# Attention by pairs of heads, with the value matmuls of four heads in four column groups

## The chip, the cores and the metric

The kernel runs on one core of one Trainium2 chip, in one launch. The metric is the device time of that launch in microseconds (us); less is better.

## The reference

One input, 4 images of 16 x 16 tokens with 192 channels (1024 tokens in all), goes through three stages, each added to its input, all in 32-bit floats:

1. a group norm, then a mixture of 8 experts (two a token, inner size 512) with a shared expert;
2. a layer norm, then attention with 12 heads of 16 channels over the 256 tokens of an image;
3. a layer norm, then a mixture of 16 experts (two a token, inner size 384) with a shared expert.

The attention, in which the change lies, takes two softmaxes, the second over the masked result of the first:

```
qkv = einsum('bnc,fc->bnf', x, w_qkv)                       # -> q, k, v
att = softmax(einsum('bhxd,bhyd->bhxy', q, k) * 16**-0.5)
att = softmax(att * mask)                                   # mask: 0.5 where x = y modulo 64, else 1
out = einsum('bhxy,bhyd->bhxd', att, v)
return einsum('bnc,oc->bno', out, w_out) + b_out
```

## The kernel before

The program is written engine by engine: each engine has one fixed order of instructions, and semaphores (`wait_ge`, `then_inc`) tie the orders together. An engine that waits holds up everything behind the wait in its own order. The order around the change is written out by hand, as a loop over steps n on each engine.

There are 48 heads (12 for each of 4 images), counted through as n. For each of them:

- `scores` (TensorE): q and k, split beforehand into high and low parts, are multiplied for two heads at once. A head's 32 rows lie in one of four row groups, and the matmuls of the two heads alternate. The result, 2 x 128 queries by 256 keys, takes one of PSUM's banks 0 to 3.
- `neg_maximum` (VectorE) takes the negated maxima of each query, `exp_scores` (ScalarE) the exponentials and their sums into one of three buffers `e1`.
- `attention` (VectorE): a reciprocal of the sums and two multiplies, which give the normalised and masked weights in one of two buffers `att`. After each a semaphore is counted up for TensorE.
- `att_transpose` (TensorE): four blocks of 128 x 128 are transposed into bank 4 or 5 by turns; the two on the diagonal as plain matmuls with the identity (L1320), the two others in the engine's own transpose mode (L1322). In the trace a plain matmul of 32-bit floats is two records, a transpose is one.
- `exp_att` (ScalarE): the exponential of the second softmax, into one of three buffers `p2_t`.
- `weigh_values` (TensorE, L1333): two matmuls, one for each half of the keys, with the head's 32 columns of values as the stationary side and 256 queries as the moving one. Head n writes partitions 32 (n mod 4) to 32 (n mod 4) + 31 of bank 6, that is, it uses one of four column groups of the array. One more column of ones gives the sum for the second softmax.

Four heads make a chunk. `out_copy` (ScalarE) takes bank 6 out; `sums_by_token` (TensorE, L1350), `invert_sums` (VectorE), a copy on GpSimd (L522), `spread_inverses` (TensorE, L1358) and `out_norm` (VectorE) divide by the sums; each third chunk `project` (TensorE, L1368) and `residual` (VectorE) finish an image. `chunk_at` says in which step a chunk's turn comes.

What each engine does in step n:

```
TensorE: scores(n+1) and (n+2) in one (n odd); att_transpose(n-2); weigh_values(n-3); chunk's parts
VectorE: neg_maximum(n); attention(n-1); chunk's parts
ScalarE: exp_scores(n); exp_att(n-2); out_copy
```

Ahead of the attention lie its layer norm, the projections to q and k (L1275) and to v (L1304); behind it the next layer norm, whose transposes (L1257) and matmuls (L1097) begin the third stage. Weights of that stage are loaded by SyncE's queue: a middle part of them is started when `sc_ps` shows that the last scores are in PSUM.

Of the kernel before, what the change touches and what calls it, by code (L numbers as in the profile page):

```python
# [29 lines left out]
P = 128  # L30
# [4 lines left out]
CH = 96  # L35
# [94 lines left out]
def build(nc, d, out):  # L130
    with ExitStack() as ctx:
# [109 lines left out]
        xn_t = sb("xn_t", [CH + 1, NCH, T])  # L241
# [53 lines left out]
        g_sh = [sb(f"g_sh{i}", [P, 512]) for i in range(2)]  # L295
# [3 lines left out]
        neg_max = sb("neg_max", [P, 4, 2])  # L299
        exp_sum = sb("exp_sum", [P, 4, 2])  # L300
        exp_inv = sb("exp_inv", [P, 2, 2])
# [3 lines left out]
        e1 = [scratch_at(512 * i, 2, TOKENS_IMG) for i in range(3)]  # L305
        att = [scratch_at(512 * (3 + i), 2, TOKENS_IMG) for i in range(2)]
        p2_t = [scratch_at(512 * (5 + i), 2, TOKENS_IMG) for i in range(3)]
# [55 lines left out]
        SUMS = 7  # L363
        TAIL = 3
        ATT_STEPS = N_HEADS + SUMS + 3 - TAIL

        def chunk_at(n, lag):


            last = N_HEADS // HPC - 1  # L370
            if lag >= SUMS and n == N_HEADS - 1 + lag - TAIL:
                return last
            c = (n - lag + 1) // HPC - 1
            return c if (n - lag + 1) % HPC == 0 and 0 <= c < last + (lag < SUMS) else None

        def sums_bank(c):

            return 0 if c == N_HEADS // HPC - 1 else 7


# [29 lines left out]
        def _(sp):  # L410
# [39 lines left out]
            sp.wait_ge(sc_ps, N_HEADS)  # L450
# [55 lines left out]
        def _(pool):  # L506
# [11 lines left out]
            for c in range(N_HEADS // HPC):  # L518
# [74 lines left out]
        def _(act):  # L593
# [32 lines left out]
            def exp_scores(n):  # L626
                act.wait_ge(nmax_ready, n + 1)
                if n >= 3:
                    act.wait_ge(att_ready, n - 2)
                for qt in range(2):  # L630
                    nc.scalar.activation(e1[n % 3][:, qt, :], bank[:, n % 4, qt * 256:(qt + 1) * 256], ACT.Exp,  # L631
                                         bias=neg_max[:, n % 4, qt:qt + 1],
                                         accum_out=exp_sum[:, n % 4, qt:qt + 1]).then_inc(e1_ready, 1)

            def exp_att(n):
                act.wait_ge(att_t_ps, n + 1)
                if n >= 3:
                    act.wait_ge(av_ps, n - 2)
                nc.scalar.activation(p2_t[n % 3][:].rearrange("p a b -> p (a b)"), bank[:, 4 + n % 2, :],
                                     ACT.Exp).then_inc(p2_ready, 1)  # L640

            def out_copy(c):

                act.wait_ge(av_ps, HPC * (c + 1))
# [28 lines left out]
        def _(dve):  # L673
# [272 lines left out]
            def neg_maximum(n):  # L946
                dve.wait_ge(sc_ps, n + 1)
                v.tensor_reduce(neg_max[:, n % 4, :], bank[:, n % 4, :].rearrange("p (a b) -> p a b", a=2),  # L948
# [12 lines left out]
            def attention(n):  # L961

                dve.wait_ge(e1_ready, 2 * n + 2)
                if n >= 2:

                    dve.wait_ge(att_t_ps, n - 1)
                go(v.reciprocal(exp_inv[:, n % 2, :], exp_sum[:, n % 4, :]))
                for qt in range(2):
                    ins = v.scalar_tensor_tensor(att[n % 2][:, qt, :], e1[n % 3][:, qt, :], exp_inv[:, n % 2, qt:qt + 1],  # L969
                                                 mask, ALU.mult, ALU.mult)  # L970
                    if qt == 0:
                        step(ins)
                ins.then_inc(att_ready, 1)

            def invert_sums(c):
                dve.wait_ge(sums_ps, c + 1)
                if c:
                    dve.wait_ge(wide_ready, c)
                v.reciprocal(o_inv[:].rearrange("p a h -> p (a h)"),   # L979
                             bank[:, sums_bank(c), 0:2 * HPC]).then_inc(inv_ready, 1)  # L980

            def out_norm(c):
# [5 lines left out]
                v.tensor_tensor(o_t[:, c % HC, :], o_raw[:, c % 2, :], bank[:, sums_bank(c), 0:TOKENS_IMG], ALU.mult  # L988
# [8 lines left out]
            for n in range(ATT_STEPS):  # L997
                if 2 <= n < N_HEADS:
                    neg_maximum(n)
                if 0 <= n - 1 < N_HEADS:  # L1000
                    attention(n - 1)
                if n == N_HEADS:

                    ln_stats(0)
                if chunk_at(n, SUMS) is not None:
                    invert_sums(chunk_at(n, SUMS))
                if n == ATT_STEPS - 1:
                    ln_rows(2, 0)
                if chunk_at(n, SUMS + 2) is not None:
                    out_norm(chunk_at(n, SUMS + 2))  # L1010
                if (chunk_at(n, SUMS + 3) or 0) % HC == HC - 1:
                    residual(chunk_at(n, SUMS + 3) // HC)
# [445 lines left out]
```

## Time and profile before

| | us |
|---|---|
| three runs | 549.63, 543.4, 545.7 |
| their median | 545.7 |
| span of the profiled execution | 538.7 |
| TensorE busy in it | 477.6 (89%) |
| VectorE busy in it | 235.1 (44%) |
| ScalarE busy in it | 162.4 (30%) |

The span goes from the first to the last instruction of one execution, taken by the hardware profiler. Its own time isn't recorded apart from it; the runs' times hold what lies around the span as well. PE is TensorE's matmuls, PEld its weight loads, DVE VectorE, ACT ScalarE, POOL GpSimd. A line such as L1333 is a line of the kernel before.

### The profile page before, as it was taken

Reading aid. Unit: us, or ns where it says so; the run is one execution under the profiler, and the core shown is the slowest. Engines: PE = TensorE matmul, PEld = TensorE weight load, DVE = VectorE, ACT = ScalarE, POOL = GpSimd, SP = SyncE. Lnnn points to the kernel's source line nnn. Section 1 sums busy time; section 2 is a strip of 40 time slices with the busy share of each in tenths; the row PEclk is TensorE's granted clock in tenths of the full one; section 3 lists DMA queues with packets and bytes.
Section 4 is the critical chain, followed back from the end, with each engine's and each line's share of the span. In section 5 each row is a group of like instructions: output and inputs, shape, how many; then the busy total and the mean of one; then the engine's idle time right before and its main releaser. Section 6 shows DMA issues by size and latency. Waiting matters only on the chain.

```text
span 538.7 us, 7851 instructions
## 1 busy us (share of the span) xinstructions
PE 477.6 (89%) x2343; PEld 322.5 (60%) x2344; DVE 235.1 (44%) x676; ACT 162.4 (30%) x418; POOL 152.3 (28%) x135
## 2 busy tenths in 40 slices
PE   0999999999998169899999999889999999999990
PEld 0554766565656147766676666655767666666660
DVE  5157232222222344676666665638623333333330
ACT  2142002111112023466656565442012111121210
POOL 2000115556655100000000000000125565566652
PEclk9999699999999669899999999999899999999996
DMA  9992111222220593000000003764211221221100
GB/s 265 209 350 67 35 52 23 39 38 35 39 27 9 141 331 135 1 1 0 2 1 1 1 2 83 181 174 112 77 38 31 33 25 26 34 35 23 12 0 0
DMA packets 20956, 36.20 MB, mean 67 GB/s; under 512 B 6544, under 2 KB 17481, under 8 KB 20484
## 3 DMA queue, kind: packets, MB, share of 16 engines
q1 hardware_dynamic: 10468, 29.56, 19.3%
q0 software_dynamic: 10464, 6.33, 8.4%
q8 instruction: 13, 0.21, 0.2%
q14 instruction: 11, 0.09, 0.1%
HBM read 31.92 MB, written 8.45 MB: 75 GB/s over the span
## 4 chain that ended last, share of the span: by engine, by line
PE 69%; DMA 15%; DVE 6%; issue 5%; ACT 1%; POOL 1%; POOLq 1%; SPq 0%; DVEq 0%
PE bank L1158 15%; DMA sum<-y,slot_tok 12%; PE bank L1333 9%; PE bank L1097 8%; PE bank L1173 6%; PE bank L1320 6%; PE bank L1127 4%; PE bank L1275 4%; PE bank L1289 3%; PE bank L1165 2%; PE bank L1322 2%; PE bank L1368 2%; PE bank L1134 1%; PE bank L1079 1%; PE bank L1304 1%
## 5 line engine op out<-in xcount | busy, mean ns | idle before, releaser
L473 POOL DMA_INDIRECT rows<-xn_rows,slot_tok x56 | 58.4, 1042 | 131.5 <-DVEq L800 90.6
L1158 PE MATMUL bank<-w_first,rows_t 96*128 x248 | 85.4, 487 | 0.2 <-issue 0.2
L1173 PE MATMUL bank<-w_second,hid_t 128*128 x370 | 71.4, 333 | 8.3 <-issue 6.3
L859 DVE TENSOR_SCALAR y<-bank,slot_w 128x192 f32<-128x192 f32 x54 | 22.6, 418 | 102.5 <-PE bank L1173 83.6
L1173 PEld LDWEIGHTS bank<-w_second,hid_t 128*128 128x128 f32 x370 | 58.7, 190 | 13.5 <-issue 13.1
L484 POOL DMA_INDIRECT out<-y,slot_tok x31 | 48.9, 1577 | 47.4 <-DMA out<-y,slot_tok 28.2
L1158 PEld LDWEIGHTS bank<-w_first,rows_t 96*128 96x128 f32 x248 | 44.6, 190 | 25.5 <-issue 0.7
L631 ACT ACTIVATE scratch<-bank,neg_max 128x256 f32<-128x256 f32 x96 | 44.6, 470 | 39.2 <-DVE neg_max L948 34.4
L1333 PE MATMUL bank<-scratch,w_first 128*32 128x256 f32 x192 | 50.9, 390 | 0.0
L522 POOL COPY act_h<-o_inv 128x256 f32<-128x256 f32 x12 | 4.8, 400 | 162.7 <-DVE o_inv L979 162.0
L484 POOL DMA_INDIRECT sum<-y,slot_tok x23 | 36.3, 1577 | 36.3 <-DMA sum<-y,slot_tok 23.7
L1152 PE MATMUL bank<-w_first,rows_t 96*128 (+1 forms) x92 | 43.4, 593 | 0.1
L1320 PE MATMUL bank<-const,scratch 128*128 128x128 f32 x192 | 42.1, 302 | 1.1 <-DVE scratch L969 1.1
L969 DVE SCALAR_TENSOR_TENSOR scratch<-scratch,exp_inv,const 128x256 f32<-128x256 f32 x96 | 42.3, 482 | 1.7
L852 DVE TENSOR_TENSOR act_h<-bank,act_g 128x384 f32<-128x384 f32 x31 | 17.3, 558 | 57.9 <-PE bank L1158 57.9
L569 ACT COPY rows_t<-bank 96x256 f32<-96x256 f32 x56 | 20.5, 365 | 64.1 <-PE bank L1134 63.8
L580 ACT ACTIVATE act_g<-bank 128x384 f32<-128x384 f32 x31 | 15.2, 490 | 75.1 <-PE bank L1158 75.1
L1320 PEld LDWEIGHTS bank<-const,scratch 128*128 128x128 f32 x192 | 29.4, 192 | 13.0 <-DVE scratch L969 5.3
L575 ACT ACTIVATE act_h<-bank 128x512 f32<-128x512 f32 x23 | 13.7, 597 | 76.7 <-PE bank L1152 76.7
L1097 PE MATMUL bank<-xn_t,w_first 96*128 96x512 f32 x64 | 31.6, 640 | 3.5 <-DVE xn_t L700 3.5
L847 DVE COPY hid_t<-bank 128x384 f32<-128x384 f32 (+1 forms) x54 | 32.9, 610 | 3.7 <-PE bank L1165 3.4
L948 DVE TENSOR_REDUCE neg_max<-bank 128x2 f32<-128x512 f32 x48 | 32.4, 676 | 2.8 <-PE bank L1289 2.3
(172 smaller groups left out, 649.3 us busy)
## 6 DMA issues: line engine op xcount, KB each, us to landing
w_first<-in_gate_up SPq DMA_DIRECT2D x16, 576.0 KB
w_second<-in_down SPq DMA_DIRECT2D x1, 4608.0 KB, 24.5
w_first<-in_fc SPq DMA_DIRECT2D x1, 3072.0 KB
w_second<-in_fc SPq DMA_DIRECT2D x1, 3072.0 KB, 28.5
xn_rows<-xn_tok SPq DMA_DIRECT2D x2, 768.0 KB, 5.9
rows<-xn_rows,slot_tok POOLq DMA_INDIRECT x56, 2.7
w_first<-in_x_t SPq DMA_DIRECT2D x2, 384.0 KB, 4.4
w_first<-in_w SPq DMA_DIRECT2D x1, 768.0 KB, 7.0
```

The source lines that it names most:

```text
L473: pool.indirect_dma_start(rows[b % 2][:], None, xn_rows[L.l], bass.IndirectOffsetOnAxis(slot_tok[:, b:b + 1].bitcast(U32), 0), bounds_chec ...
L484: pool.indirect_dma_start(target, bass.IndirectOffsetOnAxis(slot_tok[:, b:b + 1].bitcast(U32), 0), y[b % 2][:], None, bounds_check=T - 1, ...
L631: nc.scalar.activation(e1[n % 3][:, qt, :], bank[:, n % 4, qt * 256:(qt + 1) * 256], ACT.Exp, bias=neg_max[:, n % 4, qt:qt + 1], accum_out ...
L847: v.tensor_copy(hid_t[:, 0:L.I], bank[:, 7, 0:L.I]).then_inc(L.hid_t_ready, 1)
L948: v.tensor_reduce(neg_max[:, n % 4, :], bank[:, n % 4, :].rearrange("p (a b) -> p a b", a=2), AXX, ALU.max, negate=True).then_inc(nmax_rea ...
L969: ins = v.scalar_tensor_tensor(att[n % 2][:, qt, :], e1[n % 3][:, qt, :], exp_inv[:, n % 2, qt:qt + 1], mask, ALU.mult, ALU.mult)
L1097: ins = pe.matmul(bank[:, bk + s % 2, :], w[:, k, g, ic * P:(ic + 1) * P], xn_t[0:CH, k, half * HALF:(half + 1) * HALF], start=(k == 0), s ...
L1152: ins = pe.matmul(bank[:, 5, :], rows_t[0:kr, k, :], w(kr, k * I0, I0), start=(k == 0), stop=(k == NCH - 1))
L1158: ins = pe.matmul(bank[:, 5 + g, 0:I1], rows_t[0:CH, k, :], w(CH, (k * 2 + g) * I1, I1), start=(k == 0), stop=(k == NCH - 1))
L1173: ins = pe.matmul(bank[:, 1, 0:C], hid_t[:, tile(ic)], w(P, ic * C, C), start=(ic == 0), stop=(ic == L.IC - 1))
L1320: ins = pe.matmul(dst, src, ident, start=True, stop=True)
L1333: ins = pe.matmul(bank[g * HG:(g + 1) * HG, 6, 0:TOKENS_IMG], v_tok[:, 2 * img + kt, h, :], p2_t[n % 3][:, kt, :], start=(kt == 0), stop=( ...
```

## The change

Every step of the attention now treats a pair of heads, p = 0 to 23:

- `scores(p)` writes two banks, 0 and 1 or 2 and 3, and counts its semaphore once.
- `neg_maximum(p)` is one instruction over both heads' banks (1024 columns), `exp_scores(p)` four activations with one count, `attention(p)` one reciprocal and four multiplies. They write in place, into `e1`, of which there are three of twice the size; `att` is gone.
- `att_transpose(p)` transposes eight blocks into banks 4 and 5 together, with no second pair of banks; the diagonal blocks stay plain matmuls with the identity. `exp_att(p)` is one activation over both banks.
- `weigh_values(c)` does a chunk's four heads in one go: for each half of the keys the four heads one after another, each in its own column group.
- The sums of a chunk go to columns of bank 6 behind the values, and the spread inverses always to bank 7. The last chunks' parts are written out behind the loops.
- The three buffers `p2_t` of a pair lie in the scratch area, in `xn_t` (now 128 partitions high) and in the two `g_sh` as one.

What each engine does in step p is now:

```
TensorE: scores(p+2); att_transpose(p); weigh_values (p even); chunk's parts
VectorE: neg_maximum(p+2); attention(p); chunk's parts
ScalarE: exp_scores(p+2); exp_att(p); out_copy
```

The core of the diff:

```diff
-            def exp_scores(n):
-                act.wait_ge(nmax_ready, n + 1)
-                if n >= 3:
-                    act.wait_ge(att_ready, n - 2)
-                for qt in range(2):
...
+            def exp_scores(p):
+                act.wait_ge(nmax_ready, p + 1)
+                if p >= 3:
+                    act.wait_ge(att_t_ps, p - 2)
+                for q in range(4):
...
+                ins.then_inc(e1_ready, 1)
+
+            def exp_att(p):
+                act.wait_ge(att_t_ps, p + 1)
+                if p >= 3:
+                    act.wait_ge(av_ps, (p - 3) // PAIRS_CHUNK + 1)
+                nc.scalar.activation(p2_t[p % 3].rearrange("p a b -> p (a b)"),
+                                     bank[:, 4:6, :].rearrange("p a b -> p (a b)"), ACT.Exp).then_inc(p2_ready, 1)
...
             act.wait_ge(v_ps, NT // 2)
-            for n in range(N_HEADS + 3):
-                if n < N_HEADS:
-                    exp_scores(n)
-                if 0 <= n - 2 < N_HEADS:
-                    exp_att(n - 2)
-                if chunk_at(n, 3) is not None:
-                    out_copy(chunk_at(n, 3))
+            exp_scores(0)
+            exp_scores(1)
+            for p in range(N_PAIRS):
+                if p + 2 < N_PAIRS:
+                    exp_scores(p + 2)
+                exp_att(p)
+                if chunk_at(p, 1) is not None:
+                    out_copy(chunk_at(p, 1))
+            out_copy(N_CHUNKS - 1)
...
-            def attention(n):
-
-                dve.wait_ge(e1_ready, 2 * n + 2)
-                if n >= 2:
-
-                    dve.wait_ge(att_t_ps, n - 1)
-                go(v.reciprocal(exp_inv[:, n % 2, :], exp_sum[:, n % 4, :]))
-                for qt in range(2):
-                    ins = v.scalar_tensor_tensor(att[n % 2][:, qt, :], e1[n % 3][:, qt, :], exp_inv[:, n % 2, qt:qt + 1],
+            def attention(p):
+
+                dve.wait_ge(e1_ready, p + 1)
+                go(v.reciprocal(exp_inv[:, p % 2, :], exp_sum[:, p % 4, :]))
+                for q in range(4):
+                    ins = v.scalar_tensor_tensor(e1[p % 3][:, q, :], e1[p % 3][:, q, :], exp_inv[:, p % 2, q:q + 1],
                                                  mask, ALU.mult, ALU.mult)
...
+            for p in range(N_PAIRS):
+                if p + 2 < N_PAIRS:
+                    neg_maximum(p + 2)
+                attention(p)
+                if chunk_at(p, 2) is not None:
+                    invert_sums(chunk_at(p, 2))
+                if chunk_at(p, 3) is not None:
+                    out_norm(chunk_at(p, 3))
+                if (chunk_at(p, 4) or 0) % HC == HC - 1:
+                    residual(chunk_at(p, 4) // HC)
...
+            def scores(p):
+
+                pair, img = (2 * p, 2 * p + 1), 2 * p // HEADS
+                if p >= 2:
+                    pe.wait_ge(e1_ready, p - 1)
...
+            def att_transpose(p):
+                pe.wait_ge(att_ready, p + 1)
+                if p:
+                    pe.wait_ge(p2_ready, p)
+                for m in range(2):
+                    for kt in range(2):
+                        for qt in range(2):
+                            dst = bank[:, 4 + m, (kt * 2 + qt) * P:(kt * 2 + qt + 1) * P]
+                            src = e1[p % 3][:, 2 * m + qt, tile(kt)]
+                            if kt == qt:
+
+                                ins = pe.matmul(dst, src, ident, start=True, stop=True)
+                            else:
+                                ins = pe.transpose(dst, src, ident)
+                ins.then_inc(att_t_ps, 1)
+
+            def weigh_values(c):
+                pe.wait_ge(p2_ready, PAIRS_CHUNK * (c + 1))
+                if c:
+
+                    pe.wait_ge(o_raw_ready, c)
+                    pe.wait_ge(inv_ready, c)
+                img = c // HC
                 for kt in range(2):
...
+                    for g in range(HPC):
+                        p = c * PAIRS_CHUNK + g // 2
+                        ins = pe.matmul(bank[g * HG:(g + 1) * HG, 6, 0:TOKENS_IMG],
+                                        v_tok[:, 2 * img + kt, (c % HC) * HPC + g, :], p2_t[p % 3][:, 2 * (g % 2) + kt, :],
+                                        start=(kt == 0), stop=(kt == 1))
                 ins.then_inc(av_ps, 1)
...
+            for p in range(N_PAIRS):
+
+                if p + 2 < N_PAIRS:
+                    scores(p + 2)
+                att_transpose(p)
+                if chunk_at(p, 1) is not None:
+                    weigh_values(chunk_at(p, 1))
+                if chunk_at(p, 2) is not None:
+                    sums_by_token(chunk_at(p, 2))
+                if chunk_at(p, 3) is not None:
+                    spread_inverses(chunk_at(p, 3))
+                if (chunk_at(p, 4) or 0) % HC == HC - 1:
+                    project(chunk_at(p, 4) // HC)
+            weigh_values(N_CHUNKS - 1)
+            spread_inverses(N_CHUNKS - 2)
+            sums_by_token(N_CHUNKS - 1)
+            spread_inverses(N_CHUNKS - 1)
+            project(IMAGES - 1)
```

## Rows read from the trace of the kernel before

**Rows 1.** The page: an engine's busy time; a costly group of VectorE.

```profile
PE 477.6 (89%) x2343; PEld 322.5 (60%) x2344; DVE 235.1 (44%) x676; ACT 162.4 (30%) x418; POOL 152.3 (28%) x135
...
L969 DVE SCALAR_TENSOR_TENSOR scratch<-scratch,exp_inv,const 128x256 f32<-128x256 f32 x96 | 42.3, 482 | 1.7
```

**Rows 2.** Busy time by stretch: stretch, its length, busy (instructions) by engine, clock, DMA.

```profile
223.00:350.00 127.00, 124.30 (x787) 82.48 (x788) 86.22 (x233) 77.97 (x254) 4.80 (x12) 0.99 0.11 29
...
222.80:226.20 3.40, 2.13 (x22) 1.81 (x22) 2.83 (x8) 2.56 (x11) 0.00 (x0) 1.00 0.00 0
...
226.20:229.70 3.50, 3.50 (x14) 1.89 (x10) 3.43 (x10) 3.21 (x12) 0.00 (x0) 0.51 0.00 0
...
55.60:59.00 3.40, 3.40 (x11) 2.53 (x10) 0.36 (x1) 0.00 (x0) 1.04 (x1) 0.50 0.21 53
```

**Rows 3.** The chain of waits: start us, length us, what.

```profile
202.34 12.56 PE bank L1275 x54
...
261.12 0.98 PE bank L1333 x4
...
270.73 0.98 PE bank L1333 x4
271.71 2.15 PE bank L1368 x12
...
342.68 1.74 PE bank L1333 x8
```

**Rows 4.** The timeline of TensorE, one chunk: start us, length us, what.

```profile
259.15 0.44 PE L1358 MATMUL bank<-const,act_h 128*128 128x128 f32 x2
259.52 0.39 PE L1289 MATMUL bank<-k_high,q_parts 32*128 32x256 f32 x2
...
259.97 0.29 PE L1289 MATMUL bank<-k_low,q_parts 32*128 32x256 f32 x2
260.19 0.49 PE L1320 MATMUL bank<-const,scratch 128*128 128x128 f32 x2
260.51 0.38 PE L1322 MATMUL bank<-const,scratch 128*128 128x128 f32 x2
260.73 0.39 PE L1320 MATMUL bank<-const,scratch 128*128 128x128 f32 x2
261.05 1.05 PE L1333 MATMUL bank<-scratch,w_first 128*32 128x256 f32 x4
262.03 0.49 PE L1320 MATMUL bank<-const,scratch 128*128 128x128 f32 x2
...
263.87 0.61 PE L1350 MATMUL bank<-const,w_first 128*128 128x4 f32 x4
264.41 0.39 PE L1289 MATMUL bank<-k_high,q_parts 32*128 32x256 f32 x2
```

**Rows 5.** The timeline at the attention's start.

```profile
223.87 0.88 DVE L969 SCALAR_TENSOR_TENSOR scratch<-scratch,exp_inv,const 128x256 f32<-128x256 f32 x2
...
224.80 0.49 PE L1320 MATMUL bank<-const,scratch 128*128 128x128 f32 x2 [0.84 <-DVE scratch L969]
```

**Rows 6.** The timeline of VectorE in one step.

```profile
264.64 0.64 DVE L948 TENSOR_REDUCE neg_max<-bank 128x2 f32<-128x512 f32 x1
265.20 0.15 DVE L967 RECIPROCAL exp_inv<-exp_sum 128x2 f32<-128x2 f32 x1
265.39 0.88 DVE L969 SCALAR_TENSOR_TENSOR scratch<-scratch,exp_inv,const 128x256 f32<-128x256 f32 x2
```

**Rows 7.** The timeline of ScalarE in one step.

```profile
265.32 0.47 ACT L631 ACTIVATE scratch<-bank,neg_max 128x256 f32<-128x256 f32 x1 [0.97 <-DVE neg_max L948]
...
266.23 0.59 ACT L639 ACTIVATE scratch<-bank 128x512 f32<-128x512 f32 x1
```

**Rows 8.** The timeline of TensorE at the low clock.

```profile
226.39 0.79 PE L1320 MATMUL bank<-const,scratch 128*128 128x128 f32 x2
...
227.97 1.87 PE L1333 MATMUL bank<-scratch,w_first 128*32 128x256 f32 x4
```

More of the change, by code:

```diff
@@ L362, in build, with chunk_at @@
         N_HEADS = IMAGES * HEADS
[L363 to L378, printed above, removed]
+        N_PAIRS = N_HEADS // 2
+        N_CHUNKS = N_HEADS // HPC
+        PAIRS_CHUNK = HPC // 2
+        def chunk_at(p, lag):
+            c = (p - lag + 1) // PAIRS_CHUNK - 1
+            if c == N_CHUNKS - 1 or (p - lag + 1) % PAIRS_CHUNK or c < 0 or c >= N_CHUNKS:
+                return None
+            return c
+        SUMS_AT = TOKENS_IMG
         HALF = T // 2
@@ L448, in _ @@
             sp.dma_start(w_second[:], d["down"]).then_inc(s_w1b, 16)
-            sp.wait_ge(sc_ps, N_HEADS)
+            sp.wait_ge(sc_ps, N_PAIRS)
             for e in range(EARLY, MIDDLE):
@@ L516, in _ @@
             pool_blocks(pool, L0, sum0)
-            for c in range(N_HEADS // HPC):
+            for c in range(N_CHUNKS):
                 pool.wait_ge(inv_ready, c + 1)
@@ L995, in residual @@
                 dve.sem_inc(x_new, 1)
[L997 to L1012, printed above, removed]
+            for p in range(N_PAIRS):
[8 more added lines that the diff above has]
+                    residual(chunk_at(p, 4) // HC)
+            ln_stats(0)
+            out_norm(N_CHUNKS - 2)
+            invert_sums(N_CHUNKS - 1)
+            ln_rows(2, 0)
+            out_norm(N_CHUNKS - 1)
+            residual(IMAGES - 1)
             ln_stats(1)
@@ L1325, in weigh_values @@
-            def weigh_values(n):
-                img, h = n // HEADS, n % HEADS
-                g, c = n % HPC, n // HPC
-                pe.wait_ge(p2_ready, n + 1)
-                if g == 0 and c:
-                    pe.wait_ge(o_raw_ready, c)
-                for kt in range(2):
-                    ins = pe.matmul(bank[g * HG:(g + 1) * HG, 6, 0:TOKENS_IMG],
-                                    v_tok[:, 2 * img + kt, h, :], p2_t[n % 3][:, kt, :],
-                                    start=(kt == 0), stop=(kt == 1))
+            def att_transpose(p):
[12 more added lines that the diff above has]
+                ins.then_inc(att_t_ps, 1)
@@ L1340, in sums_by_token, with spread_inverses @@
                 pe.wait_ge(o_raw_ready, c + 1)
-                if sums_bank(c) == 0:
-                    pe.wait_ge(e1_ready, 2 * N_HEADS)
-                elif c and c % HC == 0:
+                for qt in range(2):
+                    o = SUMS_AT + qt * HPC
+                    ins = pe.matmul(bank[:, 6, o:o + HPC], o_raw[:, c % 2, tile(qt)], sum_row,
+                                    start=True, stop=True)
+                ins.then_inc(sums_ps, 1)
+            def spread_inverses(c):
+                pe.wait_ge(wide_ready, c + 1)
+                if c and c % HC == 0:
                     pe.wait_ge(x_new, c // HC)
@@ L1348, in sums_by_token @@
                 for qt in range(2):
-                    o = qt * HPC
-                    ins = pe.matmul(bank[:, sums_bank(c), o:o + HPC], o_raw[:, c % 2, tile(qt)], sum_row,
-                                    start=True, stop=True)
-                ins.then_inc(sums_ps, 1)
-            def spread_inverses(c):
-                pe.wait_ge(wide_ready, c + 1)
-                for qt in range(2):
-                    ins = pe.transpose(bank[:, sums_bank(c), tile(qt)], o_inv_wide[:, qt].rearrange("p g d -> p (g d)"), ident)
+                    ins = pe.transpose(bank[:, 7, tile(qt)], o_inv_wide[:, qt].rearrange("p g d -> p (g d)"), ident)
                 ins.then_inc(spread_ps, 1)
```

80 lines of the change are left out of this document (24 added, 56 removed).

## The prediction

> **What bounds the kernel now.** I began with the page's shares [rows 1]: TensorE is busy for 89% of the span. The page says nothing of which stage the change sits in, so the next view is the busy time by stretch. Between 223 and 350 us, the attention, TensorE is busy 124.30 of 127.00 us, VectorE 86.22 and ScalarE 77.97, at a granted clock of 0.99 [rows 2]. TensorE alone is the bound there, and what it does all the time must be priced step by step. The chain of waits gives the rhythm: the same value matmuls come back at 261.12 and 270.73, so a chunk of four heads takes 9.61 us [rows 3]. The timeline of TensorE then splits one such chunk [rows 4]: a pair's scores take 0.67 us to the next step (259.52 to 260.19), the six transpose records of one head 0.86 (to 261.05), the value matmuls of one head 0.98 (to 262.03), the sums 0.54 (263.87 to 264.41) and the spreading of the inverses 0.37 (259.15 to 259.52). 2 x (0.67 + 2 x 0.86 + 2 x 0.98) + 0.54 + 0.37 = 9.61: the pieces fill the period, and there is no hole in it. A projection adds 2.15 us once for each image [rows 3].
>
> Why there is no hole matters more than the sizes. In the loop before, TensorE transposes head n-2 in the step in which VectorE normalises head n-1, and the scores are two to three heads ahead of the maxima. Each engine works on something that the other finished a step ago.
>
> **What the change takes away on TensorE.** Transposes: twelve records in a row instead of twice six, so one change of kind of work less. A pair of records costs 0.22 us (260.51 to 260.73 [rows 4]), so twelve take 0.86 + 6 x 0.11 = 1.52 against 1.72: 0.2 us a pair is gained.
>
> Values: the same sixteen records a chunk, two for each matmul (four for the two matmuls of a head in the row at 261.05). One costs 1.74 / 8 = 0.218 us [rows 3], and the switch 0.98 - 4 x 0.218 = 0.11. No row shows two column groups at work at once, so the cost is bounded. One after the other: 16 x 0.218 + 0.11 = 3.60 us a chunk, against 3.92 now. All four at once: 4 x 0.218 + 0.11 = 0.98. The nearest rows are those of the scores, whose pairs lie in two row groups: four couples of 256-column matmuls start within 0.45 us (259.52 to 259.97, three steps of 0.15 a couple [rows 4]), while 96-row matmuls of 512 columns in the same number format take 12.56 / 54 = 0.233 us each, 0.116 for 256 columns and 0.233 for two [rows 3]. So two groups do run at once. But the order matters: each value matmul is two records in the same column group, one behind the other, and matmuls start in order. The second record of group 0 has to wait for the first, group 1 can then join it, and so on: at most two at once, 9 slots for 16 records, 9 x 0.218 + 0.11 = 2.07 us. I take that, as it follows from the rows of the scores, and keep both ends for the range.
>
> The page "TensorEngine Tiling (Array Packing)" of the Trainium skill (Theoretical Speedup) gives up to four times for 32 columns. By it the values would cost 0.98 us a chunk, 1.09 less than in my sum.
>
> On TensorE alone a chunk would be 2 x (0.67 + 1.52) + 2.07 + 0.91 = 7.36 us, a gain of 2.25 us in each of twelve. That is the gain the page of the profile invites one to book, and I don't think that it comes.
>
> **What the change adds: a loop through two engines with no step of slack.** Follow the new order. In step p TensorE issues the scores of pair p+2, then the transposes of pair p. VectorE in step p takes the maxima of pair p+2, then normalises pair p. The maxima wait for those scores. The transposes of p wait for the normalisation of p, which stands behind the maxima of p+2 in VectorE's order. The scores of p+3 stand behind the transposes of p in TensorE's order. So: transposes of p, scores of p+3, maxima of p+3, normalisation of p+1, transposes of p+1. Nothing of this overlaps. TensorE waits during all of VectorE's part and VectorE waits during all of TensorE's; the value matmuls, sums, spreads and projections stand between transposes and scores and lie wholly on the path, too. One pair's round, with the clock at 2.4 GHz:
> - scores, first start to last end: 259.52 to 259.97 + 0.29 = 0.74 us [rows 4];
> - handing over to VectorE and back 0.05 each (normalisation 223.87 + 0.88 = 224.75, transposes at 224.80 [rows 5]);
> - maxima of 1024 columns: 0.56 for 512 (264.64 to 265.20 [rows 6]), and the further 512 columns at no more than that; 1.10;
> - reciprocal to first multiply 0.19 (265.20 to 265.39 [rows 6]), then four multiplies: two take 0.88 in all [rows 6], one alone 0.48 [rows 1], so each further one adds 0.40: 0.88 + 2 x 0.40 = 1.68;
> - transposes 1.52.
> Sum 0.74 + 0.10 + 1.10 + 0.19 + 1.68 + 1.52 = 5.33 us a pair, 10.7 a chunk before values, sums and spreads, where all of it takes 9.61 now.
>
> Start: the first transposes are at 224.80 [rows 5]. They now come after two more exponentials (0.91, half of a pair's four, 265.32 to 266.23 [rows 7]), a pair's scores (0.79 with the handover), the maxima (1.10) and two more multiplies (0.80): 228.4. From there 23 rounds to the last transposes: 21 x 5.33 = 111.9; two without scores and maxima, 2 x 3.44 = 6.9; eleven times values, 22.8; eleven sums, 5.9; ten spreads, 3.7; three projections, 6.5. Together 157.7, so they start at 386.1. Before they start at 342.68 - 0.86 = 341.8 [rows 3]. The tail behind them grows by 0.66 (six more records), 0.35 (one exponential over both heads; four exponentials of 256 columns and one of 1024 are some 2.8 us a pair and hidden in the loop) and 0.3 (2.07 instead of 1.74): 1.3. At full clock the span grows by 44.3 + 1.3 = 45.6 us.
>
> **The clock.** The start of the attention is a small picture of the new loop: from 222.8 to 226.2 us TensorE does scores, waits 0.84 us for a normalisation, transposes; it is busy 2.13 of 3.40 us, and in the next stretch its granted clock is 0.51, that is 1.2 GHz [rows 2, 5]. In the new loop it waits 3.1 us of every 5 to 8. I expect the clock to fall over and over. How quickly it returns is open: one fully busy stretch sufficed after 226.2, while from 55.6 to 59 us it stayed at 0.50 with TensorE busy 3.40 of 3.40 [rows 2]. At the low level six transpose records take 1.58 instead of 0.86 (226.39 to 227.97) and four value records 1.87 instead of 1.05 [rows 8]. Then the scores cost 1.14, the twelve transposes 2.9, the round 7.11, the short round 4.82, the values 4.1, sums, spreads and projections twice theirs: 149.3 + 9.6 + 45.1 + 19.2 + 12.9 = 236.1 instead of 157.7, with 6.7 more in the tail: 85 us on top if nothing ran at 2.4 GHz. A chunk has one long busy stretch (transposes, values, spread, scores: some 9 us at the low level), in which the clock should return, and two pauses, in which it falls. I take six tenths of TensorE's work at the low level: 45.6 + 0.6 x 85 = 97 us. This share is a choice between the ends, not a reading.
>
> **Parts that cost nothing.** Normalising in place, dropping the separate buffers, the wider rooms for two tensors and single increments change no term. The load of the middle experts' weights waits for the last scores as before, and is covered by the same 40 us of routing and shared expert behind the attention; without that cover it would be as late as now. The bank that holds a pair's transposes is no longer doubled: its exponential, near 0.95 us, is done during scores and VectorE's part (3.9 us). ScalarE has 2.8 us of work in a round of 5.3.
>
> **The sum.** The profiled execution's span is 538.7 us, 7.0 below the median of 545.7 of the three runs; what lies around the span doesn't change, so the difference is added to the median: 545.7 + 97 = 643 us.
>
> **Rivals.**
> 1. The clock holds, because the pauses are short: 545.7 + 45.6 = 591. For it: the attention's granted clock was 0.99 over 127 us, and no row shows what the clock does when short pauses and bursts alternate for long. Against it: the start of this very stage [rows 2]. 0.25.
> 2. It falls once and stays low: 545.7 + 131 = 677. For it the stretch at 55.6. 0.13.
> 3. The column groups don't overlap at all: 1.5 us more a chunk at full clock, 3 at low, about 27 more than my forecast: 670. 0.08. Four at once: 1.1 to 2.2 less a chunk, 623. 0.08.
> 4. The other side: TensorE passes a waiting matmul, and starts the scores of pair p+3 while the transposes of pair p still wait. Then the loop is cut, TensorE's 7.36 us a chunk (above VectorE's 2 x (1.10 + 0.19 + 1.60) + 0.6 = 6.4, the 0.6 being the two short steps that a chunk has beside its pairs) set the time, and the gain is 2.25 x 11 = 25 us: 521. It decides as soon as the scores can go before the wait. No row shows a matmul that started ahead of an earlier one; weight loads do stand ahead of matmuls. 0.04. The page "TensorE: Matmul & The Clock Gate" of the Trainium skill (Part 3, What overlaps and what doesn't) says that matmuls start and end strictly in order, which speaks against this one.
> My forecast has the remaining 0.42.
>
> **Range and chances.** 585 to 688 takes in rival 1 with its nearest variants, rivals 2 and 3, and leaves out the fourth and the corner of four groups at once with a full clock (578). A difference under 1% can't be told from none here (the three runs spread over 6 us). Faster by over 1%: 0.03; within 1%: 0.02, for a mixture of small pauses that I can't construct; slower: 0.95.
>
> **What will show it.** TensorE's busy share in the attention falls from 98% to some 55 to 65%, and nearly all of its idle time ends with the normalisation's multiply; VectorE's idle time ends with the scores. The chain of waits shows VectorE with a third or more of the attention, where it hardly appears now. The attention lasts 170 to 255 us. If value records of different groups start in pairs 0.22 us apart, two at once is right; if a chunk's sixteen start within 1 us, four. The granted clock should show many changes between the levels. I am wrong if scores are seen to start before the waiting transposes, or if the clock stays at one level throughout.

## The result and the profile after

The changed kernel takes 627.0 us (median of four runs), against 547.7 for the kernel before beside it: a ratio of 1.149 (95% interval 1.142 to 1.157), slower by 15%. Here and below the medians take in all executions; some executions of one and the same kernel have a lower granted clock throughout and take 1 to 3% longer, and the ratios leave these out. The profiled execution took 625.9 us, with a span of 623.8.

The page of the changed kernel, its engines' totals, the granted clock and the shares of the chain that ended last:

```profile
PE 485.3 (78%) x2343; PEld 346.7 (56%) x2344; DVE 231.4 (37%) x628; ACT 161.0 (26%) x394; POOL 152.5 (24%) x135
...
PEclk9998799999985955787966676666999999999997
...
PE 60%; DVE 16%; DMA 15%; issue 6%; ACT 2%; POOLq 1%; POOL 0%; SPq 0%; DVEq 0%
```

TensorE has the same 2343 matmul records as before [rows 1] and is busy 8 us longer, yet the span is 85 us longer. So most of the time went into waiting. VectorE holds 16% of the last chain, 6% before, and the clock row has a ragged middle. The busy time of the whole attention and of its first 34 us (stretch, length, busy time and instructions by engine, clock, DMA):

```profile
223.00:430.00 207.00, 129.37 (x789) 104.91 (x788) 82.29 (x184) 76.85 (x230) 4.83 (x12) 0.68 0.08 18
...
223.00:257.00 34.00, 20.35 (x109) 17.11 (x108) 12.72 (x25) 13.89 (x48) 0.00 (x0) 0.54 0.00 0
```

TensorE is busy 129.37 of 207 us where it was 124.30 of 127 [rows 2], and the granted clock is 0.68 instead of 0.99. Everything behind the attention is as before: the next stage's first matmul stands at 351.51 before and at 436.85 now, 187 us from the end of the span in both. The chain of waits of the changed kernel shows the loop that the prediction spelt out, here from the value matmuls of one chunk through the next transposes, and the value matmuls a chunk later:

```profile
298.91 1.00 PE bank L1340 x16
299.91 0.37 PE bank L1362 x2
300.28 0.69 PE bank L1293 x8
...
300.99 1.22 DVE neg_max L955
302.21 0.10 DVE exp_inv L971
...
302.74 1.28 DVE scratch L973 x3
...
304.06 0.49 PE bank L1325 x2
...
314.23 1.86 PE bank L1340 x16
```

Values, spread inverses, scores, maxima, reciprocal, multiplies, transposes follow each other (the first multiply is in a row left out). Nothing overlaps: in the timeline TensorE is idle for 3.11 us before the transposes at 304.06, and VectorE for 4.39 us before 300.32, when the inverses are spread. Compare the chunk at 261.12 [rows 3], where the value matmuls ended the waits and VectorE didn't appear. The list of waits says the same from both sides:

```profile
PE bank L1325 <- DVE scratch L973: 73.6, 24, 3.2
DVE w_first L992 <- PE bank L1362: 49.7, 10, 5.5
...
DVE o_inv L983 <- PE bank L1350: 37.0, 12, 3.7
...
DVE neg_max L955 <- PE bank L1293: 22.4, 21, 5.9
```

TensorE waits for the normalisation in each of the 24 rounds, 3.1 us on average. VectorE's waits are for the spread inverses, the sums and the scores, all made by TensorE in the same step.

The values are where the profile disagrees with the prediction. TensorE's timeline of one chunk:

```profile
298.84 0.41 PE L1340 MATMUL bank<-scratch,w_first 128*32 128x256 f32 x2
298.85 0.41 PE L1340 MATMUL bank<-xn_t,w_first 128*32 128x256 f32 x2
299.08 0.38 PE L1340 MATMUL bank<-scratch,w_first 128*32 128x256 f32 x2
299.09 0.39 PE L1340 MATMUL bank<-xn_t,w_first 128*32 128x256 f32 x2
```

Each row holds two records; `scratch` and `xn_t` hold the inputs of the chunk's two pairs. Four records, one for each head, start within 0.02 us and the next four 0.24 us later: four column groups at once, not two. The chain row at 298.91 gives 1.00 us for sixteen records, and 1.86 at the low clock (314.23).

### The profile page after: what moved, and what is told of

It reads as the page before. It is cut to its first block, busy times and chain, and to the rows that moved or that the text cites. A ratio compares the mean times of both kernels' runs of the same rounds, so it can differ in the third digit from the quotient of the medians.

```text
span 623.8 us, 7662 instructions
## 1 busy us (share of the span) xinstructions
PE 485.3 (78%) x2343; PEld 346.7 (56%) x2344; DVE 231.4 (37%) x628; ACT 161.0 (26%) x394; POOL 152.5 (24%) x135
## 4 chain that ended last, share of the span: by engine, by line
PE 60%; DVE 16%; DMA 15%; issue 6%; ACT 2%; POOLq 1%; POOL 0%; SPq 0%; DVEq 0%
PE bank L1162 12%; DMA sum<-y,slot_tok 12%; PE bank L1325 8%; PE bank L1101 7%; DVE scratch L973 5%; PE bank L1177 5%; DVE neg_max L955 4%; PE bank L1293 3%; PE bank L1327 3%; PE bank L1279 3%; PE bank L1340 3%; PE bank L1131 3%; PE bank L1372 2%; PE bank L1169 2%; PE bank L1308 1%
## 5 line engine op out<-in xcount | busy, mean ns | idle before, releaser
L1325 PE MATMUL bank<-const,scratch 128*128 128x128 f32 x192 | 57.1, 424 | 73.6 <-DVE scratch L973 73.6
L1325 PEld LDWEIGHTS bank<-const,scratch 128*128 128x128 f32 x192 | 46.2, 313 | 79.3 <-DVE scratch L973 79.3
L973 DVE SCALAR_TENSOR_TENSOR scratch<-scratch,exp_inv,const 128x256 f32<-128x256 f32 x96 | 40.2, 481 | 0.8
L955 DVE TENSOR_REDUCE neg_max<-bank 128x4 f32<-128x1024 f32 x24 | 29.3, 1224 | 26.0 <-PE bank L1293 26.0
L1169 PE MATMUL bank<-const,act_h 128*128 128x128 f32 x185 | 29.7, 276 | 1.0 <-ACT act_h L578 0.5
```

The costliest lines, as they stand in the source:

```text
L955: v.tensor_reduce(neg_max[:, p % 4, :], bank[:, b:b + 2, :].rearrange("p b (a k) -> p (b a) k", a=2), AXX, ALU.max, negate=True).then_inc( ...
L973: ins = v.scalar_tensor_tensor(e1[p % 3][:, q, :], e1[p % 3][:, q, :], exp_inv[:, p % 2, q:q + 1], mask, ALU.mult, ALU.mult)
L1169: ins = pe.transpose(bank[:, 7, tile(ic)], act_h[:, tile(ic)], ident)
L1325: ins = pe.matmul(dst, src, ident, start=True, stop=True)
```

## The experiments

All times are medians; each ratio is to the kernel before, run on the same chip beside it.

**The tie undone: `e1_swap`.** VectorE's order, one exchange:

```diff
             for p in range(N_PAIRS):
+                attention(p)
                 if p + 2 < N_PAIRS:
                     neg_maximum(p + 2)
-                attention(p)
```

> The changed kernel with one edit in VectorE's loop: the normalisation of pair p stands before the maxima of pair p+2, not behind them. The computation is the same. Theory A (the loss is the loop without slack, in which TensorE and VectorE take turns): the round is cut, because the maxima of p+2 then run beside the transposes of p. VectorE's own work is 1.14 + 0.20 + 1.68 = 3.0 us a pair and 0.3 for a chunk's parts, TensorE's 3.15, ScalarE's 3.0, so a round should take 3.3 to 4.2 us instead of 8.1, the clock should stay up, and the time should be 515 to 545 us. Theory B (the loss is that the transposes have one pair of banks, so that they wait for the second exponential): the edit changes nothing on that path, rounds stay above 5.3 us and the time over 590 us. Theory C (TensorE's own work in the new form is slower): no change, 620 or more.

Measured: 564.2 us, ratio 1.029 (1.023 to 1.034). The direction is theory A's, and B and C are out: one call moved, no work removed, and 63 us are gone. The size is short of what was expected: the range ended at 545 us, 19 us below the median and 14 below the two executions that the ratio rests on (559.2 and 559.4). Its waits in the attention (us in total, times, longest):

```profile
PE bank L1325 <- DVE scratch L973: 31.1, 19, 2.7
DVE w_first L992 <- PE bank L1362: 28.3, 10, 4.4
DVE o_inv L983 <- PE bank L1350: 19.5, 11, 3.7
DVE x_tok L997 <- PE bank L1372: 6.9, 3, 2.7
```

The last three: 28.3 + 19.5 + 6.9, some 55 us in which VectorE still waits for a chunk's parts that TensorE makes behind the transposes of the same step. The granted clock is 0.78 in the attention (235 to 370 us), where it was expected to stay up. The exchange had cut one tie of several.

**The clock alone: `e2_filler`.** The changed kernel with useless work in TensorE's pauses:

```diff
                     scores(p + 2)
+                    if p:
+                        pe.wait_ge(p2_ready, p)
+                    for _ in range(10):
+                        pe.matmul(bank[:, 4, 0:P], ident, ident, start=True, stop=True)
                 att_transpose(p)
```

> The changed kernel with ten plain matmuls of 128 x 128 on the identity put in front of each wait for the normalisation, into a bank that the transposes overwrite: some 2.2 us of work inside a pause of 3.1 us, which nothing waits for. It gives results as before. Theory A (about half of the loss is the clock, which falls because of the pauses): the granted clock in the attention rises from 0.68 to over 0.9, the way from the first to the last transposes shrinks from 187 to 146 us (111.9 + 6.9 + 11 x 0.98 + 5.9 + 3.7 + 6.5), and the time is 580 to 592 us, still slower than before by the loop alone. Rival (the clock is low for another reason, or the low clock is hidden by VectorE's part): the clock stays under 0.8 and the time over 610 us, or rises by the filler.

Measured: 589.8 us, ratio 1.085 (1.079 to 1.090), as theory A had it. More work on TensorE makes the kernel 37 us faster, because the clock stays up for most of the attention. The busy time of the attention and, from the chain, the beginnings of three chunks:

```profile
235.00:400.00 165.00, 144.06 (x1213) 123.02 (x1212) 81.31 (x183) 74.35 (x220) 4.82 (x12) 0.93 0.09 23
```

```profile
265.14 1.00 PE bank L1340 x16
...
277.60 1.00 PE bank L1340 x16
...
290.07 1.00 PE bank L1340 x16
```

The clock is 0.93, and a chunk takes 12.46 to 12.47 us. The prediction's terms, with the values at 1.00, give 2 x 5.33 + 1.00 + 0.91 = 12.57. From the first transposes (240.14) to the last (387.78) are 147.6 us, where 146 were expected.

**The order of the groups: `e3_group_outside`.**

```diff
-                for kt in range(2):
-                    for g in range(HPC):
+                for g in range(HPC):
+                    for kt in range(2):
```

> The changed kernel with the two loops of the value matmuls exchanged: all matmuls of one head, so of one column group, and then the next head's. Same results. Theory A1 (column groups take work independently of the program's order, as four groups started within 0.02 us although each matmul is two records of the same group): nothing changes, a chunk's sixteen records still take 1.0 us at full clock, time 622 to 632 us. Theory A2 (they start in program order, and it is the alternation of groups that lets four run at once): the values cost 2.8 to 3.6 us a chunk at full clock and up to twice that at the low one, 20 to 55 us more in all, 647 to 680 us.

Measured: 624.3 us, ratio 1.148 (1.142 to 1.153), no different from the changed kernel's. The chain still has sixteen records in 1.89 us at the low clock:

```profile
278.07 1.89 PE bank L1340 x16
...
294.93 1.89 PE bank L1340 x16
```

The records of the two pairs run side by side, though the program now gives all eight of the first pair's before any of the second's. The view of the line in the chunk at 294.93:

```profile
L1340 PE MATMUL bank<-scratch,w_first x8: 634/634/636, 294.9 to 296.1; 128*32 128x256 f32 x8
L1340 PE MATMUL bank<-xn_t,w_first x8: 634/634/636, 294.9 to 296.2; 128*32 128x256 f32 x8
```

So the program's order of heads doesn't decide here: matmuls of a later column group start beside those of an earlier one. Theory A1 stands, and the prediction's reasoning that matmuls start in order falls for different column groups.

**Values alone: `e4_values_alone`.** The kernel before, head by head, with `weigh_values` of the change every fourth step and seven buffers for its input:

```diff
-                if 0 <= n - 3 < N_HEADS:
-                    weigh_values(n - 3)
+                if chunk_at(n, 3) is not None:
+                    weigh_values(chunk_at(n, 3))
...
-                    act.wait_ge(av_ps, n - 2)
+                    act.wait_ge(av_ps, (n - 7) // HPC + 1)
```

> The kernel before with one part of the change alone: the value matmuls of four heads at once, every fourth step, with seven buffers for the second exponentials (four of them in the rooms that the change uses) and everything else head by head in its old order. Same results. Theory A (the column groups are worth what they save on TensorE, and only the loop spoils it): a chunk loses 3.92 - 0.98 = 2.9 us on TensorE, which comes down to 6.7; VectorE with 7.2 us of work a chunk is then the bound, so 2.2 us a chunk are gained, 26 in all: 515 to 525 us, the loop's clock staying near 1. Rival (values in one go don't help because other engines take the place of TensorE at once, or the clock falls as TensorE pauses): 540 to 550 us.

Measured: 528.6 us, ratio 0.972 (0.969 to 0.975). One part of the change, without the new loop, is faster than the kernel before. The beginnings of three chunks in its chain and the attention's busy time:

```profile
250.32 1.00 PE bank L1335 x16
...
258.14 1.00 PE bank L1335 x16
...
265.96 1.00 PE bank L1335 x16
```

```profile
243.00:334.00 91.00, 79.35 (x727) 62.12 (x725) 75.66 (x208) 69.36 (x228) 4.80 (x12) 1.00 0.15 38
```

A chunk takes 7.82 us instead of 9.61. VectorE is busy 75.66 of 91 us and TensorE 79.35; the expected 7.4 us a chunk was a little too good, as neither is ever wholly busy, and the time is 3.6 us above the expected 515 to 525, well below the rival's 540.

**The other ties: `e5_late_parts`.** VectorE's loop again, a chunk's parts a step behind TensorE's:

```diff
-            for p in range(N_PAIRS):
-                if p + 2 < N_PAIRS:
-                    neg_maximum(p + 2)
-                attention(p)
-                if chunk_at(p, 2) is not None:
-                    invert_sums(chunk_at(p, 2))
...
+            for p in range(N_PAIRS + 1):
+                if p < N_PAIRS:
+                    attention(p)
+                if chunk_at(p - 1, 2) is not None:
+                    invert_sums(chunk_at(p - 1, 2))
...
+                if p + 2 < N_PAIRS:
+                    neg_maximum(p + 2)
```

> The changed kernel with VectorE's loop in the order normalisation of pair p, then the chunk's parts (inversion, output product, residual) that TensorE prepared in the step before, then the maxima of pair p+2. Same results. In the run with the exchange alone VectorE still waited 48 us in the attention for the sums, the spread inverses and the projections of its own step; here each of them has a step's time. Theory A (ties between TensorE and VectorE within one step are what costs, and nothing else limits a round above some 3.5 us): a chunk takes 6.9 to 7.6 us, the attention some 90 us from the first to the last transposes, the time is 520 to 540 us, below that of the kernel before. Rival (the one pair of banks for the transposes, or ScalarE's order with the first exponentials of p+2 ahead of the second of p, limits the round): a chunk stays over 9 us and the time over 550 us.

Measured: 525.8 us, ratio 0.963 (0.953 to 0.973). Theory A's range was met, and the pair form with the same instructions is faster than the kernel before by 4%, 100 us faster than as it was changed. The chunk's length was missed: 7.89 us at full clock (299.02 to 306.91 in its chain) and 9.24 (281.62 to 290.86) with a pause in it, where 6.9 to 7.6 were expected. The rival had something in it. Two of TensorE's waits, and the chain where it still pauses:

```profile
PE bank L1326 <- ACT xn_t L643: 6.8, 5, 1.8
PE bank L1326 <- ACT g_sh L643: 3.6, 3, 1.8
```

```profile
275.81 1.24 DVE neg_max L955
...
277.44 0.72 ACT scratch L634 x4
...
278.34 0.66 ACT scratch L634 x3
279.00 0.92 ACT g_sh L643
...
280.06 0.46 PE bank L1326 x2
```

Maxima of p+2, then its four first exponentials (the trace has further records for reading out their sums, so the rows count seven), behind them the second exponential of p (0.92 us, at 279.00), then the transposes of p+1. The first exponentials of p+2 stand before the second of p in ScalarE's order, and the one pair of banks keeps the transposes of p+1 waiting for it.

**The tie put into the kernel before: `e6_old_tied`.**

```diff
-                if n % 2 and n + 1 < N_HEADS:
-                    scores(n + 1)
-                if 0 <= n - 2 < N_HEADS:
-                    att_transpose(n - 2)
+                if n % 2 == 0 and 2 <= n < N_HEADS:
+                    scores(n)
+                if 0 <= n - 1 < N_HEADS:
+                    att_transpose(n - 1)
```

> The kernel before, head by head, with the tie of the change put in: TensorE's scores of heads n and n+1 stand in the even step n, in which VectorE takes the maxima of n, and the transposes are those of head n-1, which VectorE normalises in the same step. Nothing else is moved, same results. Theory A (the tie is the cause, whatever the form of the value matmuls and however wide the steps): in each even step TensorE waits for one maxima and one normalisation, 1.7 to 1.8 us, a pair takes some 6.0 us instead of 4.8, 24 x 1.2 = 29 us more, and with the clock falling at times 570 to 595 us. Rival (the pair form or the value matmuls in one go are what slows the changed kernel): 545 to 552 us.

Measured: 697.0 us, ratio 1.282 (1.269 to 1.295). The cause is confirmed from the other side, with the old value matmuls and the old widths; the size was missed by over 100 us. Two things had been left out. The chunk's parts (sums, L1350, and spread inverses, L1358) are tied in the same way in the other steps, so that TensorE waits for VectorE in nearly every step and not in every second one. And the clock is 0.61 in the attention:

```profile
PE bank L1320 <- DVE scratch L969: 71.0, 38, 2.1
DVE o_inv L979 <- PE bank L1350: 37.6, 9, 4.5
```

```profile
223.00:490.00 267.00, 188.17 (x736) 113.70 (x735) 80.68 (x207) 73.94 (x244) 3.62 (x9) 0.61 0.02 5
```

**The same with the clock held: `e10_old_tied_filler`.** The kernel of `e6_old_tied`, with six plain matmuls on the identity before each wait for a normalisation:

```diff
             def att_transpose(n):
-                pe.wait_ge(att_ready, n + 1)
                 if n >= 2:
                     pe.wait_ge(p2_ready, n - 1)
+                for _ in range(6):
+                    pe.matmul(bank[:, 4 + n % 2, 0:P], ident, ident, start=True, stop=True)
+                pe.wait_ge(att_ready, n + 1)
```

> The kernel of e6_old_tied with six plain matmuls on the identity, 1.3 us, before each wait for a normalisation, into the bank that the transposes then overwrite. Same results. e6_old_tied came out at 697 us where 570 to 595 were expected, with a granted clock of 0.61 in the attention, and with the chunk's parts tied within a step as well. Theory: the tie costs 8.2 us a pair at full clock (scores 0.74, twice 0.86 and 0.98, twice 1.7 on VectorE, 0.4 of parts) against 4.8, 80 us in all, and the clock the rest: with the clock held the time is 615 to 640 us. Rival (the clock is only a companion, or the tie costs more by itself): over 670 us.

Measured: 628.3 us, ratio 1.160 (1.141 to 1.179), within the theory's 615 to 640. The clock is 1.00:

```profile
223.00:420.00 197.00, 181.08 (x1272) 137.10 (x1271) 79.74 (x203) 72.27 (x239) 3.62 (x9) 1.00 0.01 3
```

So of some 150 us that the tie cost the kernel before, 69 (697.0 - 628.3) are the low clock and 82 (628.3 - 546.3) the tie; the two runs were on different chips. This kernel's 628 and the changed kernel's 627 are alike by chance: the one has a full clock, the other a low one.

**Less work on the diagonal: `e7_all_transposed`.** `e5_late_parts` with `pe.transpose` for the diagonal blocks too.

```diff
-                            if kt == qt:
-
-                                ins = pe.matmul(dst, src, ident, start=True, stop=True)
-                            else:
-                                ins = pe.transpose(dst, src, ident)
+                            ins = pe.transpose(dst, src, ident)
```

> The kernel of e5_late_parts with the diagonal blocks transposed in TensorE's transpose mode too, one record instead of two: four records, 0.44 us, less on TensorE for a pair. Same results. If VectorE or a wait between engines bounds the round in e5_late_parts, the time stays within 4 us of it; if TensorE bounds it, 8 to 10 us less; if plain matmuls on the diagonal keep the clock up, it falls more often here and the time is equal or more in spite of less work.

Measured: 533.1 us, ratio 0.967 (0.955 to 0.979), which can't be told from the 0.963 of `e5_late_parts`. Ten microseconds less of TensorE's records bought nothing that can be measured. The granted clock of the whole span was lower, 0.91 against 0.93 to 0.94 in the runs that the ratio rests on, so the third case that was named (plain matmuls keep the clock up) is not excluded, and neither is the first. This stays open.

**ScalarE's order, and the start: `e8_second_exp_first` and `e9_start`.** The first exchanges two lines of `e5_late_parts`, the second also moves `neg_maximum(1)` behind the copies of v:

```diff
+                exp_att(p)
                 if p + 2 < N_PAIRS:
                     exp_scores(p + 2)
-                exp_att(p)
```

```diff
             neg_maximum(0)
-            neg_maximum(1)
...
+            neg_maximum(1)
```

> The kernel of e5_late_parts with one more edit, in ScalarE's loop: the second exponential of pair p stands before the first ones of pair p+2. Same results. In e5_late_parts TensorE's transposes of p+1 wait some 1.75 us in every other chunk or so for the second exponential of p, which stands behind four activations in ScalarE's order. Theory (now the one pair of banks for the transposes is what comes last): these waits go, five or so of 1.75 us, 8 to 12 us in all with the clock falling less: 512 to 520 us. Rival (the first exponentials then come too late for the normalisation of p+2, so the wait moves to VectorE): 522 to 530 us.

> The kernel of e8_second_exp_first with VectorE's maxima of pair 1 moved behind its four copies of v. Same results. Those copies free the banks in which TensorE makes v; in the changed kernel the two wide maxima (2.4 us) stand before them, TensorE pauses and the clock fell there, 220 us into the run, for 34 us. Theory: TensorE's pause before v shrinks by 1.2 us and the clock stays up or returns sooner, 2 to 8 us less than e8. Rival: the pause is bounded by something else, time within 2 us of e8.

Measured: 515.6 us, ratio 0.950 (0.939 to 0.962), and 512.5 us, ratio 0.945 (0.934 to 0.957; one of its six executions took 897 us, which nothing here explains). The first lies in the expected 512 to 520. By the ratios alone it can't be told from `e5_late_parts`, as the two intervals overlap; the traces can: at full clock a chunk takes 7.89 us there and 6.75 here (250.18 to 256.93), and TensorE's waits for the second exponential, 6.8 and 3.6 us there, are gone from its list. The second edit can't be told from none. The beginnings of three chunks in the chain of `e9_start`, and the attention's busy time:

```profile
246.00 1.00 PE bank L1341 x16
...
252.75 1.00 PE bank L1341 x16
...
259.50 1.00 PE bank L1341 x16
```

```profile
225.00:318.00 93.00, 82.16 (x775) 66.52 (x774) 80.52 (x183) 73.17 (x230) 4.80 (x12) 0.98 0.14 33
```

A chunk takes 6.75 us against 9.61 before [rows 3]. VectorE is busy for 80.52 of 93 us and TensorE for 82.16, at a clock of 0.98.

## Why the prediction came out right

643 us were forecast and 627 measured. The mechanism that the forecast rests on was right, one term of its sum was wrong, and the share of low clock was luck. Step by step:

- **The loop without slack.** Right, and shown three times: undoing it takes 63 us (`e1_swap`) and, with the chunk's parts, 101 (`e5_late_parts`) from the changed kernel; putting it into the kernel before costs 149 (697.0 - 548.4) (`e6_old_tied`). Its price was right as well: with the clock held, a chunk takes 12.47 us where the terms give 12.57. The maxima take 1.14 us (300.99 to 302.13) instead of the 1.10 assumed. Rival 4 is out: the transposes of every round waited, and no scores were seen ahead of waiting transposes. (Its chance, 0.04, doesn't go with the 0.03 that the prediction gave to a faster kernel.)
- **The clock.** It falls again and again, as the main case had it. Rivals 1 and 2 are out: the stretch's mean is 0.68. From the first transposes (234.63) to the last (421.82) are 187.2 us. The prediction's sums, with the values as measured, are 146 at full clock and 212 at low (1.00 and 1.86 for the values instead of 2.07 and 4.1), so 0.62 of TensorE's extra was paid; the mean granted clock over these 187 us, 0.69, agrees (low for 0.62 of the time). The 0.6 in the forecast was a choice, and a lucky one; nothing in the profile before gave it. `e2_filler` shows the clock's part apart from the loop: 37 us.
- **The value matmuls.** The step that failed: "at most two at once, 9 slots for 16 records, 9 x 0.218 + 0.11 = 2.07 us". It is four at once, 1.00 us at full clock, and `e3_group_outside` shows that the order of the heads in the program doesn't matter. This is the second half of rival 3, which had a chance of 0.08 and the price of 623 us. The term was too high by 11 x (0.38 x 1.07 + 0.62 x 2.24) = 20 us, the largest error. The page "TensorEngine Tiling (Array Packing)" of the Trainium skill (Theoretical Speedup, Key Properties) had it right with up to four times for 32 columns and tiles that run independently; the trace agrees, with 1.00 us against the 3.60 of sixteen records one after the other. The prediction set it aside for a rule of order. Such a rule stands in the page "TensorE: Matmul & The Clock Gate" of the Trainium skill (Part 3, What overlaps and what doesn't), which has all matmuls start and end in the program's order. The starts measured here decide against it for matmuls in different groups.
- **The start.** The first transposes were put at 228.4 and stand at 234.63. Of these 6 us, 1.9 come from the work ahead (the first scores stand at 216.30 before and at 218.23 now; in the other profiles they stand anywhere from 212.8 to 223.3). The rest goes with the clock, which was low during the matmuls for v and the first rounds (0.54 from 223 to 257 us, the second stretch above). This is chance in part: in the profiles of `e1_swap` and `e8_second_exp_first`, whose program is the same up to the end of these matmuls, the granted clock in the 10 us from the first scores is 0.97 and 0.98, in the changed kernel's 0.61. What tips it isn't shown; `e9_start` moved work in that place and couldn't be told from its neighbour.
- **The tail.** 9.65 us from the last transposes to the next stage's first matmul became 15.0; the prediction had 1.3 and at the low clock up to 6.7 more, so the 5.4 measured are what it expected.
- **The base.** The prediction took the 7.0 us between the span of the profiled execution (538.7) and the median as what lies around the span. Where a run has both numbers, that is some 2.1 us (625.88 and 623.8 here); the other 5 mean that the profiled execution was faster than the three timed ones. With 20 us too much for the values, 5 too much here, 6 too little for the start and 2 too little for the clock (0.02 x 85), the forecast is some 17 too high; 16 were measured.
- **What cost nothing.** Right for the in-place multiplies and the loads. The single pair of banks for the transposes was hidden in the slow loop, as said, but only there: once the ties were gone it came last (`e5_late_parts`), and 10 us of the medians, 1.14 in each chunk, hung on it together with ScalarE's order.

The gain that TensorE's sum promised was real: 2.25 us a chunk, or 3.32 with the values as measured (1.00 instead of 2.07). `e9_start` collects 2.86 of it. The change as made hid it behind the loop.

## What to carry to other kernels

When engines with orders written by hand are regrouped, write down for each step which engine waits for whom within the same step: two such waits in opposite directions put both engines' work end to end here, and what TensorE had saved was lost behind it. Take each operation from what was made a step earlier, chunk's parts and all, and cut the ties one by one, since the next one comes last as soon as the first is gone. A pause in TensorE can cost more than its length: here 37 of 79 us were the clock, and useless matmuls in the pauses won them back.

## What was not expected of the hardware

- TensorE didn't keep the program's order between column groups, or between row groups. The four groups' records in the chunk above start within 0.02 us although each group has two behind one another for each matmul, and in `e3_group_outside` the second pair's start with the first pair's. At the start of the attention the program gives all eight score matmuls of pair 0 first and then those of pair 1, in the other two row groups; the trace has them four abreast:

```profile
218.23 0.41 PE L1293 MATMUL bank<-k_high,q_parts 32*128 32x256 f32 x4 [1.41 <-DVE k_low L949]
218.45 0.31 PE L1293 MATMUL bank<-k_low,q_parts 32*128 32x256 f32 x4
218.57 0.32 PE L1293 MATMUL bank<-k_high,q_parts 32*128 32x256 f32 x4
218.69 0.31 PE L1293 MATMUL bank<-k_low,q_parts 32*128 32x256 f32 x4
```

- A larger busy share of TensorE didn't go with a higher granted clock: the tied kernel before had 0.61 with TensorE busy for 70% of the stretch (188.17 of 267 us), the changed kernel 0.68 with 62% (129.37 of 207). The low clock itself lengthens the busy time, so the two shares don't compare the work done; what sets the clock between such loops isn't shown.
